# The last stage's up products: half of the contraction split into rounded fp32r parts, row buffers moved over dead weights

## The reference, cut to what matters

```python
# x2: 3200 tokens x 256;  E = 16 experts, 4 per token, hidden width 256
for e in range(E):
    we = sum(weights * (indices == e))                    # routing weight, 0 for tokens not sent to e
    h = silu(x2 @ W1[e].T + b1[e]) * (x2 @ W3[e].T + b3[e])
    y = y + (h @ W2[e].T + b2[e]) * we[:, None]
out = x + tanh(g_ffn[1]) * y
```

## Time and profile before

| | |
|---|---|
| median of 3 runs | 2079.4 us (2075.22 to 2079.53) |
| time of the profiled execution | 2076.01 us |
| its span | 2074.3 us |
| last stage in the span | about 1704 to 2074 us |
| TensorE, busy share of the span | 93% |
| VectorE, busy share of the span | 64% |
| mean granted TensorE clock | 0.963 |

### The profile page before, as it was taken

One profiled execution on the slowest core, in us unless ns is written; L12 is line 12 of the kernel. 1 busy time (PEld: TensorE's weight loads), 2 busy tenths in 40 slices (PEclk: granted clock), 3 DMA queues, 4 the chain that ended last, 5 costly groups with the idle time before them and its releaser, 6 DMA issues. The chain is left out here.

```text
span 2074.3 us, 39938 instructions
## 1 busy us (share of the span) xinstructions
PE 1929.3 (93%) x11418; PEld 1345.2 (65%) x11418; DVE 1329.4 (64%) x4051; ACT 930.3 (45%) x2321; POOL 1144.8 (55%) x1374
## 2 busy tenths in 40 slices
PE   6999999999999579999959999999999839999997
PEld 4777777777777368888825555555555525666664
DVE  4777777777777642223237888888888735555555
ACT  2444444444343423333237666666676514333332
POOL 2344444444444344444446888888888733555555
PEclk9999999999999689999979999999999859999999
DMA  5211111010107013333311111111111954555554
GB/s 143 58 41 27 41 28 40 28 41 28 41 28 265 9 37 52 52 52 52 53 33 32 56 53 54 49 52 54 52 57 49 319 174 67 90 92 87 93 92 74
DMA packets 138406, 142.24 MB, mean 69 GB/s; under 512 B 31658, under 2 KB 128658, under 8 KB 137816
## 3 DMA queue, kind: packets, MB, share of 16 engines
q1 hardware_dynamic: 98586, 92.90, 14.9%
q0 software_dynamic: 37888, 44.51, 13.3%
q10 hardware_dynamic: 1726, 2.28, 0.4%
HBM read 89.88 MB, written 51.94 MB: 68 GB/s over the span
## 5 line engine op out<-in xcount | busy, mean ns | idle before, releaser
L864 POOL TENSOR_SCALAR prob<-prob,rc 100x363 f32<-100x363 f32 x256 | 157.5, 625 | 344.9 <-DVE rc L689 344.9
L1881 POOL DMA_INDIRECT out<-y,xr x115 | 178.6, 1553 | 196.0 <-DVE y L1914 120.1
L1985 PE MATMUL psG<-expert_w,xgT 128*128 x460 | 220.3, 602 | 1.3 <-ACT xgT L1948 1.1
L1086 PE MATMUL psJ<-wkv,cTn 96*121 96x512 f32 x384 | 177.6, 599 | 0.0
L1623 POOL DMA_INDIRECT acc<-y,slots x57 | 90.3, 1584 | 136.9 <-DVE y L1682 123.9
L603 ACT ACTIVATE prob<-psS,nm 100x361 f32<-100x361 f32 x256 | 141.6, 561 | 54.0 <-DVE nm L684 47.9
L1898 DVE TENSOR_TENSOR pre<-psG,late 128x512 f32<-128x512 f32 x115 | 79.6, 692 | 128.7 <-PE psG L1985 112.5
L684 DVE TENSOR_REDUCE nm<-psS 100x2 f32<-100x722 f32 x128 | 115.1, 899 | 71.0 <-PE psS L498 70.9
L1536 POOL DMA_INDIRECT rows<-row,pos_of x128 | 137.1, 1071 | 35.6 <-issue 28.4
L1659 DVE TENSOR_TENSOR hid<-psU,gate 128x512 f32<-128x512 f32 x57 | 39.4, 691 | 159.6 <-PE psU L1775 159.6
L1948 ACT ACTIVATE xgT<-psX 128x256 f32<-128x256 f32 x115 | 44.1, 383 | 207.1 <-PE psX L1976 167.5
(11 more groups left out here) (306 smaller groups left out, 5093.6 us busy)
## 6 DMA issues: line engine op xcount, KB each, us to landing
xr<-rows SPq DMA_DIRECT2D x115, 136.5 KB
expert_w<-in_L_ffn_moe_w SPq DMA_DIRECT2D x8, 1024.0 KB
late<-in_ctx SPq DMA_DIRECT2D x32, 181.5 KB
cT<-in_ctxT SPq DMA_DIRECT2D x32, 180.5 KB
cT<-in_ctxT SPq DMA_DIRECT2D x64, 90.2 KB
expert_w<-in_L_ffn_moe_w SPq DMA_DIRECT2D x8, 512.0 KB
expert_w<-in_L_ffn_W1T SPq DMA_DIRECT2D x16, 256.0 KB
expert_w<-in_L_ffn_W3T SPq DMA_DIRECT2D x16, 256.0 KB
```

The lines of the kernel that those rows point to most:

```text
L864: g.tensor_scalar(prob[:, q, :], prob[:, q, :], rc[:, q:q + 1], 1.0, ALU.mult, ALU.mult).then_inc(prob_done, 1)
L1086: mm = t.matmul(ph[0:rows, 0:cols], lhs, wt[:, k, :], start=k == 0, stop=k == 1)
L1881: g.indirect_dma_start(acc, bass.IndirectOffsetOnAxis(row_token[:, j % RING, :], 0), y[:, j % 4, :], None, compute_op=ALU.add).then_inc(sc ...
L1985: mm = t.matmul(psG[:, r, :], xT[:, r, k, :], w13[:, bass.ds(e, 1), k, :], start=k == 0, stop=k == 1)
```

## The change

For the first channel half (k = 0) the up product of the last stage is made of three fp32r matmuls: x_hi by w_hi, x_hi by w_lo, x_lo by w_hi. The second half (k = 1) stays one float32 matmul. For this:

- at the stage's start ScalarE rounds the k = 0 halves of all weights into `w_hi`, in four instructions of 128x2048, and VectorE writes the difference over the weights, also in four; TensorE waits for the fourth before `up(0)`;
- for each tile ScalarE makes two copies of 128x128 (`x_hi`, rounded, and `xT`) instead of one of 128x256, and VectorE gets one subtraction of 128x128 more (`low`), placed ahead of `biased` in its loop; TensorE waits for it ahead of the last of the up matmuls, and the next transposes wait for it too;
- `psX` takes two banks, one for each half;
- silu works in place in `pre`, and the tile `gate` goes;
- `xr` and `pre` are laid over the attention weights, which nothing reads any more.

```diff
-            wq1=sb("wq1", [P, 2, I1]), wkv1=sb("wkv1", [CK, 2, 2 * I1]), wlkv1=sb("wlkv1", [P, 2, 2 * I1]),
+            dead_at=nc.sbuf_base, wq1=sb("wq1", [P, 2, I1]), wkv1=sb("wkv1", [CK, 2, 2 * I1]), wlkv1=sb("wlkv1", [P, 2, 2 * I1]),
...
-        xr = sb("xr", [P, RING, ROW])
-        xT = sb("xgT1", [P, 2, 2, P])
-        pre = sb("pre1", [P, 2, 2 * F])
+        w_hi = sb("w13_hi1", [P, E, 2 * F], F32R)
+        xr = nc.alloc_sbuf_tensor_at("xr", [P, RING, ROW], F32, offset=c["dead_at"])
+        pre = nc.alloc_sbuf_tensor_at("pre1", [P, 2, 2 * F], F32, offset=c["dead_at"] + 4 * RING * ROW)
+        x_hi, x_lo, xT = sb("x_hi1", [P, 2, P], F32R), sb("x_lo1", [P, 2, P], F32R), sb("xT1", [P, 2, P])
...
 VectorE
+                def low(j):
+                    v.wait_ge(x_high, j + 1)
+                    v.tensor_tensor(x_lo[:, j % 2, :], psX[:, 0, 0:P], x_hi[:, j % 2, :].bitcast(F32), ALU.subtract).then_inc(x_low, 1)
...
-                        v.wait_ge(g_out, j - 1)
+                        v.wait_ge(hid_done, j - 1)
...
-                    v.tensor_tensor(hid[:, j % 2, :], pre[:, j % 2, F:2 * F], gate[:, j % 2, :], ALU.mult).then_inc(hid_done, 1)
+                    v.tensor_tensor(hid[:, j % 2, :], pre[:, j % 2, F:2 * F], pre[:, j % 2, 0:F], ALU.mult).then_inc(hid_done, 1)
...
+                for q in range(4):
+                    v.wait_ge(w_high, q + 1)
+                    v.tensor_tensor(w13[:, 4 * q:4 * q + 4, 0, :].bitcast(F32R), w13[:, 4 * q:4 * q + 4, 0, :],
+                                    w_hi[:, 4 * q:4 * q + 4, :].bitcast(F32), ALU.subtract).then_inc(w_low, 1)
                 e_of = [expert(j) for j in range(2)]
+                low(0)
...
                 for j in range(NT):
                     if j + 1 < NT:
+                        low(j + 1)
                         biased(j + 1, e_of[j + 1])
...
 ScalarE
-                    s.activation(xT[:, j % 2, :, :], psX[:, 0:2 * P].rearrange("p (k n) -> p k n", k=2), ACT.Copy).then_inc(x_out, 1)
+                    s.activation(x_hi[:, j % 2, :], psX[:, 0, 0:P], ACT.Copy).then_inc(x_high, 1)
+                    s.activation(xT[:, j % 2, :], psX[:, 1, 0:P], ACT.Copy).then_inc(x_out, 1)
...
-                    s.activation(gate[:, j % 2, :], pre[:, j % 2, 0:F], ACT.Silu).then_inc(g_out, 1)
+                    s.activation(pre[:, j % 2, 0:F], pre[:, j % 2, 0:F], ACT.Silu).then_inc(g_out, 1)
...
+                s.wait_ge(c["experts1_loaded"], 16 * W1_LOADS)
+                for q in range(4):
+                    s.activation(w_hi[:, 4 * q:4 * q + 4, :], w13[:, 4 * q:4 * q + 4, 0, :], ACT.Copy).then_inc(w_high, 1)
...
 TensorE
                     if j >= 1:
+                        t.wait_ge(x_low, j)
                         t.wait_ge(x_out, j)
...
-                    for k in range(2):
-                        mm = t.matmul(psG[:, r, :], xT[:, r, k, :], w13[:, bass.ds(e, 1), k, :], start=k == 0, stop=k == 1)
-                    mm.then_inc(g_mm, 1)
+                    hi, lo = w_hi[:, bass.ds(e, 1), :], w13[:, bass.ds(e, 1), 0, :].bitcast(F32R)
+                    t.matmul(psG[:, r, :], xT[:, r, :], w13[:, bass.ds(e, 1), 1, :], start=True, stop=False)
+                    t.matmul(psG[:, r, :], x_hi[:, r, :], hi, start=False, stop=False)
+                    t.matmul(psG[:, r, :], x_hi[:, r, :], lo, start=False, stop=False)
+                    t.wait_ge(x_low, j + 1)
+                    t.matmul(psG[:, r, :], x_lo[:, r, :], hi, start=False, stop=True).then_inc(g_mm, 1)
...
                 x_transpose(0)
+                t.wait_ge(w_low, 4)
                 up(0, expert(0))
```

More of the change, by code:

```diff
@@ L93, in build @@
             expert_w=sb("expert_w", [P, 3 * E0 * 2 * F0]),
-            wq1=sb("wq1", [P, 2, I1]), wkv1=sb("wkv1", [CK, 2, 2 * I1]), wlkv1=sb("wlkv1", [P, 2, 2 * I1]),
+            dead_at=nc.sbuf_base, wq1=sb("wq1", [P, 2, I1]), wkv1=sb("wkv1", [CK, 2, 2 * I1]), wlkv1=sb("wlkv1", [P, 2, 2 * I1]),
             wo1=sb("wo1", [P, 2, D]), wr1=sb("wr1", [P, 2, E1]), bo1=sb("bo1", [N, D]),
-            cx_g=sb("cx_g", [CK, 2]), cx_b=sb("cx_b", [CK, 2]), lt_g=sb("lt_g", [P, 2]), lt_b=sb("lt_b", [P, 2]),
+            dead_end=nc.sbuf_base, cx_g=sb("cx_g", [CK, 2]), cx_b=sb("cx_b", [CK, 2]), lt_g=sb("lt_g", [P, 2]), lt_b=sb("lt_b", [P, 2]),
             qk_g=sb("qk_g", [P, 2]), qk_s=sb("qk_s", [P, 1]),
@@ L101, in build @@
         )
+        c["dead_bytes"] = c["dead_end"] - c["dead_at"]
         c["wk0"] = c["expert_w"][:, 0:2 * I0].rearrange("p (k n) -> p k n", k=2)
@@ L1851, in experts1 @@
         sb, ps, sem = maker(stack)
-        psX, psG, psH, psD = ps("psX1", [P, 512]), ps("psG1", [P, 2, 512]), ps("psH1", [P, 512]), ps("psD1", [P, 2, 512])
-        xr = sb("xr", [P, RING, ROW])
-        xT = sb("xgT1", [P, 2, 2, P])
-        pre = sb("pre1", [P, 2, 2 * F])
+        psX, psG, psH, psD = ps("psX1", [P, 2, 512]), ps("psG1", [P, 2, 512]), ps("psH1", [P, 512]), ps("psD1", [P, 2, 512])
+        w_hi = sb("w13_hi1", [P, E, 2 * F], F32R)
+        xr = nc.alloc_sbuf_tensor_at("xr", [P, RING, ROW], F32, offset=c["dead_at"])
+        pre = nc.alloc_sbuf_tensor_at("pre1", [P, 2, 2 * F], F32, offset=c["dead_at"] + 4 * RING * ROW)
+        assert 4 * (RING * ROW + 4 * F) <= c["dead_bytes"]
+        x_hi, x_lo, xT = sb("x_hi1", [P, 2, P], F32R), sb("x_lo1", [P, 2, P], F32R), sb("xT1", [P, 2, P])
         b2, b13 = bias_views(c)
-        gate, hid, hT = sb("gate1", [P, 2, F]), sb("hid1", [P, 2, F]), sb("hT1", [P, 2, KF, P])
+        hid, hT = sb("hid1", [P, 2, F]), sb("hT1", [P, 2, KF, P])
         yb, y = sb("yb1", [P, 2, D]), sb("y1", [P, 4, D])
@@ L1864, in experts1 @@
         x_out, g_out, h_out = sem("x_out1"), sem("g_out1"), sem("h_out1")
+        x_high, x_low = sem("x_high1"), sem("x_low1")
+        w_high, w_low = sem("w_high1"), sem("w_low1")
         pre_done, hid_done, yb_done, y_done = sem("pre_done1"), sem("hid_done1"), sem("yb_done1"), sem("y_done1")
@@ L1973, in x_transpose @@
                     if j >= 1:
+                        t.wait_ge(x_low, j)
                         t.wait_ge(x_out, j)
                     for k in range(2):
-                        mm = t.transpose(psX[:, k * P:(k + 1) * P], xr[:, j % RING, k * P:(k + 1) * P], ident[:, :])
+                        mm = t.transpose(psX[:, k, 0:P], xr[:, j % RING, k * P:(k + 1) * P], ident[:, :])
                     mm.then_inc(x_mm, 1)
```

## The result

The changed kernel takes 2142.4 us (median of 4 runs, 2140.28 to 2152.11) against 2077.3 us of the kernel before on the same chip: ratio 1.032, 95% interval 1.030 to 1.035. The forecast was 2087. The direction was right; eight times as much was lost as forecast.

What follows compares the result with a forecast made beforehand. It took TensorE, busy 100 of 100 us, to bound the last stage. Steady tiles -1.5, VectorE's late steps +4, stage start +5.5 make +8 us: 2084 on the profiled 2076.0, 2087 on the median 2079.4; range 2072 to 2100.

Steps and rivals of the forecast that it cites:

- TensorE's work per tile: Last stage: one float32 product (0.86 us) removed, three fp32r matmuls (0.69) added, so 3.02 us becomes 2.85.
- The ring through VectorE: Last stage, once per tile: last up matmul, `pre`, `yb`, `y`, `hid`, `low`, next last up matmul; 3.01 us, setting the pace.
- step 3: On VectorE, start of `hid` to start of `low`: 0.33 us, upper bound 0.42.
- The fp32r weight loads: Ahead of fp32r matmuls on TensorE: 0.19 us, like float32; a skill rule on fast loads would save some 0.08.
- -0.01 x 112: Last stage's steady part: change per tile times 112 steady tiles, given as about -1.5 us.
- Rivals: Four alternative outcomes: TensorE sets the pace (0.10), shorter VectorE ring (0.15), longer ring (0.10), lower TensorE clock (0.05).
- TensorE keeps the pace: Last stage: `low` comes in time, the tile is 2.85 us; -13.5 us in all, 2066; chance 0.10.
- The clock: TensorE pauses in every tile; granted clock at half for one tile in ten, +31 us more, 2118; chance 0.05.
- The start: Last stage's beginning: rounding and subtracting weights delays `up(0)` by 6.5 us; net +5.5, bounds +4.5 and +8.
- VectorE's late moments: Last stage: VectorE steps late in some 22 of 115 tiles, 4.6 us excess, no longer swallowed by slack; taken as +4.

## Why the prediction was wrong

- *TensorE's work per tile*, 2.85 us: right. The runs with one read and `x_lo` early show 2.86.
- *The ring through VectorE*, 3.01 us: its parts were right, the sum 0.06 too long. `hid` to `x_lo` is 0.33 and `x_lo` 0.29, as forecast; the end of `x_lo` to its weight load is 0.06, not the 0.14 of the earlier trace rows, and by itself the ring is 2.95. `hid` takes 0.42 and `x_lo` starts after 0.33, so the upper bound of step 3 did not come. The passage of the Trainium skill that it went with, "VectorE: DVE Perf Modes", section "The DRAIN you can't avoid", itself says "A next op that is not held starts earlier", which the prediction left out and the trace agrees with. The fp32r weight loads stayed at 0.19 us. (A slip besides: -0.01 x 112 is -1.1 and not -1.5.)
- *What I let follow the wait* is the step that failed. The text says that TensorE "stands about 0.16 us per tile ahead of its last up matmul", and takes the next transposes as following without cost. I asked what is queued behind `low` on VectorE, where the change adds an instruction, but not what is queued behind the new wait on TensorE. Two reads of expert numbers stand there, and they make 1.45 us from the end of `x_lo` to the transposes. They turned a ring of 3.01 us per tile into one of 6.98 us per two tiles. That is +0.48 x 115 = 55 us, nearly all of the miss: 2142 - 2087 = 55, or 57 against the 2077.3 that the kernel before took in the same session, where the forecast reads 2085.
- *Rivals.* None of the four had this; "TensorE keeps the pace" has exactly this hidden condition, that the sequencer is through with its reads by the time the transposes are due. The clock stayed at 1.00.
- *The start*, +6.1 us at the first `pre` (6.5 less the 0.4 of the first up; the other 0.6 of the net +5.5 was for the second tile): measured +7.0. The rounding and the rests were right to 0.1 us. ScalarE began 0.72 ahead of SyncE's first load instead of 0.96, which is 0.24 of the 0.9 missing. TensorE began 0.8 after the last rest instead of 0.14 (1716.77 against about 1715.96), because its read of the first expert number stands behind that wait too (its load is on record at 1716.0), and that is the rest. The same step, missed a second time.
- *VectorE's late moments*, +4 us: in the changed kernel the mean tile (3.54) lies 0.03 above the median of two (3.51), 3 us in 115 tiles. Consistent, not shown by itself.

## What to carry to other kernels

A new wait can cost more than the time until it is met: register reads and address computations that used to run under the work ahead of it are exposed behind it. When a wait is added or moved later in a stream, list what the sequencer has to do between it and the next piece of work on that engine, and move the reads ahead of the wait. Then do the same for the wait in front of that, since the reads are now behind it; here that one, for `xT`, took over. In a trace the mark of it is idle time with "issue" as its releaser that keeps a fixed distance, not from the instruction in front, but from the end of whatever met the wait. The view of the read's source line then shows when the sequencer was at it.

## What the runs showed of the hardware

- One read of a number from SBUF into a TensorE register, with its bounds check, takes about 0.65 us of the sequencer; the load in it takes 0.30 in most tiles and up to 0.69 in some (the kernel in which both TensorE reads and VectorE's stand early). A tile's two reads are invisible in the dense stream of the kernel before; behind the new wait they cost 49 us.
- A wait met in time is not free: one in the kernel before cost 45 us.
- An engine's sequencer can set the pace although neither it nor the engine is always busy, and no busy share shows it: with both reads between the wait for `xT` and the last up matmul the floor was 2.90 us per tile, with 0.50 us of rest for the sequencer in the tile shown; with one read it was 2.85, TensorE's own work.
